# An attention and expert kernel: gathered rows turned by DMA instead of by TensorE, with a new order of the last two feed-forward units

## What is computed

```python
x = x + xattn_ffn(layernorm(x), ctx)   # causal self-attention, attention on ctx,
                                       # feed-forward 256 -> 1024 -> 256 (ReLU), each with add + layernorm
h = layernorm(x)
probs = softmax(h @ wg.T)              # 8 experts
topk_w, topk_idx = top_k(probs, 2);  topk_w /= sum(topk_w)
h1, h3 = h @ w1[e], h @ w3[e]          # 256 -> 512
y_e = (silu(h1) * h3) @ w2[e]          # 512 -> 256
x = x + sum over the two experts of topk_w * y_e
```

## Time and profile before

| | |
|---|---|
| median of 3 runs | 536.51 us (534.71 to 536.86) |
| profiled execution | 538.54 us, of it span 536.7 us |
| PE busy | 500.5 us (93%) |
| PEld | 326.6 us (61%) |
| DVE | 378.5 us (71%) |
| ACT | 286.5 us (53%) |
| POOL | 288.0 us (54%) |
| expert tiles, from the first ups | from 353.50 us on |

### The profile page before, as it was taken

The page is one execution under the profiler, slowest core; times in us unless marked ns, Lnnn a source line. Parts: engine busy times, 40 slices in busy tenths (PEclk is TensorE's granted clock), DMA queues, the critical chain, the costliest instruction groups (busy, mean ns, idle before and its releaser), DMA issues.

```text
span 536.7 us, 10988 instructions
## 1 busy us (share of the span) xinstructions
PE 500.5 (93%) x3686; PEld 326.6 (61%) x3686; DVE 378.5 (71%) x968; ACT 286.5 (53%) x574; POOL 288.0 (54%) x324
## 2 busy tenths in 40 slices
PE   7999999999899999898999988899998999999990
PEld 3676766666667666566666764556655656666660
DVE  6899887588877678858977989788857544444440
ACT  4556867655648637654647557455544334433430
POOL 4464112004724519936696875343566665766663
PEclk9899999999999999999999999899999999999996
DMA  8002534246887357763697770226885677878973
GB/s 278 7 31 70 171 94 120 84 107 118 145 173 143 109 110 132 160 165 109 106 213 158 145 259 11 69 65 124 142 155 100 116 120 136 126 126 123 139 91 40
DMA packets 135314, 65.61 MB, mean 122 GB/s; under 512 B 109757, under 2 KB 126590, under 8 KB 135262
## 3 DMA queue, kind: packets, MB, share of 16 engines
q1 hardware_dynamic: 127774, 54.69, 45.9%
q0 software_dynamic: 7488, 10.23, 12.8%
HBM read 28.19 MB, written 10.35 MB: 72 GB/s over the span
## 4 chain that ended last, share of the span: by engine, by line
PE 51%; DVE 16%; DMA 11%; issue 8%; ACT 6%; POOL 4%; POOLq 2%; SPq 1%; DVEq 0%; ACTq 0%
PE ps L1197 41%; DMA out<-y,qst 6%; DMA probT<-prob 3%; PE ps L1292 3%; PE ps L1294 3%; PE ps L1293 3%; DVE cmax L1735 2%; ACT ps L1008 1%; POOL y L935 1%; DVE tT L1944 1%; POOLq L955 1%; DVE prob L1876 1%; DVE arena L394 1%; POOL out L961 1%; DVE arena L468 1%
## 5 line engine op out<-in xcount | busy, mean ns | idle before, releaser
L1197 PE MATMUL ps<-arena,probT 128*128 128x256 f16 (+2 forms) x1092 | 179.6, 318 | 3.5 <-DMA probT<-prob 2.2
L1197 PEld LDWEIGHTS ps<-arena,probT 128*128 128x128 f16 (+1 forms) x1092 | 104.8, 97 | 60.7 <-issue 7.0
L961 POOL DMA_INDIRECT out<-y,qst x39 | 62.7, 1608 | 23.6 <-DMA out<-y,qst 12.9
L1197 PE MATMUL ps<-arena,qT 128*128 128x512 f16 (+1 forms) x384 | 68.9, 332 | 1.6 <-DVE prob L1876 1.2
L1007 ACT ACTIVATE prob<-ps,nbias 128x512 f16<-128x512 f32 x64 | 39.0, 609 | 53.3 <-DVE nbias L1741 53.3
L2296 DVE SCALAR_TENSOR_TENSOR ps<-ps,w1m 128x512 f32<-128x512 f32 x39 | 27.4, 703 | 53.5 <-ACT w1m L1138 51.0
L1138 ACT ACTIVATE w1m<-ps 128x512 f32<-128x512 f32 x39 | 23.3, 597 | 76.9 <-PE ps L1197 63.8
L1197 PE MATMUL ps<-arena,tT 128*128 x468 | 57.3, 273 | 0.6 <-DVE tT L2395 0.6
L776 POOL TENSOR_TENSOR rstd<-veps,expo 128x1 f32<-128x1 f32 x16 | 9.2, 573 | 88.0 <-DVE veps L1770 88.0
L1197 PEld LDWEIGHTS ps<-arena,qT 128*128 128x128 f16 x384 | 32.4, 97 | 37.1 <-issue 3.2
L1197 PE MATMUL ps<-w2s,tT 128*128 128x256 f16 x384 | 47.6, 274 | 3.4 <-DVE tT L1944 3.0
(11 more groups left out here) (232 smaller groups left out, 920.4 us busy)
## 6 DMA issues: line engine op xcount, KB each, us to landing
stage<-we_in SPq DMA_DIRECT2D x33, 256.0 KB, 3.1
prob<-we_in SPq DMA_DIRECT2D x15, 256.0 KB, 3.7
xin<-x_in SPq DMA_DIRECT2D x16, 128.0 KB, 2.8
out<-y SPq DMA_DIRECT2D x16, 128.0 KB
hrow<-tT SPq DMA_DIRECT2D x4, 512.0 KB, 3.3
y<-x_in SPq DMA_DIRECT2D x3, 512.0 KB, 7.2
stage<-z_in SPq DMA_DIRECT2D x4, 256.0 KB, 5.5
prob<-w_in SPq DMA_DIRECT2D x4, 256.0 KB, 2.8
```

Of the source, the lines that this page charges most:

```text
L961: g.indirect_dma_start(out[:rows_of(p), :], bass.IndirectOffsetOnAxis(ridx[:, n:n + 1], 0), ys[:, n % RING, :], None, compute_op=ALU.add). ...
L1197: r = t.matmul(o, lhs(a), rhs(b), start=first and n == 0, stop=last and n == 2)
```

## The change

Gathered rows are no longer turned by PE and copied by ACT: SP issues a DMA transpose of 128x512 float16 (`x_turn(n)`) into a ring of four slots in `w1m`, where the feed-forward weights lay. Because of that, the first four turns wait for the last `up`. In SP's order `x_turn(n + 4)` stands ahead of `act_turn(n)`. `gather(n)` waits for `x_turn(n - 4)`, `e_ups(n)` for `x_turn(n)`. AHEAD is 8, but gathers of a new phase wait for iteration 3 and 11, and one iteration issues two at most. In the feed-forward of blocks 2 and 3, PE's and DVE's order is rewritten, and `h_trans(2)` and `logits(2)` stand behind the last `down` and behind `e_ups(0)`.

```diff
-RING, AHEAD, BEHIND = 4, 6, 3
-LEAD = 2
+RING, AHEAD, BEHIND = 4, 8, 3
+GATHERS_FROM = {1: 3, 2: 11}
+MOST = 2
...
-        xT = ph[:, 4096:5120].rearrange("p (q b c) -> p q b c", q=2, b=2 * KD)
+        xT = w1m[:, 2 * NI:].bitcast(F16).rearrange("p (s b c) -> p s b c", s=RING, b=2 * KD)
...
+            def x_turn(n):
+
+                s = n % RING
+                if n < RING:
+                    wait(sp, "f_up", KF * NB)
+                else:
+                    wait(sp, "e_up", n - RING + 1)
+                wait(sp, f"e_x{s}", 16 * (n // RING + 1))
+                sp.dma_start_transpose(xT[:, s], xg[:, s, :]).then_inc(sm[f"e_t{s}"], 16)
+
...
             store_h(sp, 2)
+            for n in range(RING):
+                x_turn(n)
             for n in range(NJ):
+                if n + RING < NJ:
+                    x_turn(n + RING)
                 if n < NJ - 1:
                     act_turn(n)
...
-                    wait(pool, "e_xtr", n - RING + 1)
+                    wait(pool, f"e_t{n % RING}", 16 * (n // RING))
...
-            issued = AHEAD - 1
+            issued = 5
             for n in range(NJ):
-                while issued < min(NJ, n + AHEAD + (LEAD if n > PHASES[2][1] - AHEAD + 1 else 0)):
-                    gather(issued)
-                    issued += 1
+                for _ in range(MOST):
+                    if issued < min(NJ, n + AHEAD) and n >= GATHERS_FROM.get(phase_of(issued), 0):
+                        gather(issued)
+                        issued += 1
...
-                    if u == NB - 1 and f == 6:
-                        h_hi(2)
...
             ffn(NB - 1)
+            h_hi(2)
-
-            def x_copy(n, q):
-                act_.wait_ge(sm["e_xtr"], n + 1)
-                copy(xT[:, q, :, :].rearrange("p b c -> p (b c)"), x_bank(n)).then_inc(sm["e_xcp"], 1)
...
-            def x_trans(n, s):
-                pe.wait_ge(sm[f"e_x{s}"], 4 * (n - s) + 16)
-                for b in range(2 * KD):
-                    r = t.transpose(x_bank(n)[:, b * P:(b + 1) * P], xg[:, s, b * P:(b + 1) * P],
-                                    ident16[:])
-                r.then_inc(sm["e_xtr"], 1)
...
-                pe.wait_ge(sm["e_xcp"], n + 1)
+                s = n % RING
+                pe.wait_ge(sm[f"e_t{s}"], 4 * (n - s) + 16)
...
-            make_lists(0)
             down(3, 2)
             up(3, 5)
             down(3, 3)
             up(3, 6)
+            make_lists(0)
             down(3, 4)
...
             down(3, 7)
-            logits(2)
+            wait(pe, "r_list", 1)
+            h_trans(2, 0)
+            h_trans(2, 1)
             wait(pe, "f_lo", KF * NB)
             wait(pe, "st_lo", G_FF + len(rest))
-            wait(pe, "e_xcp", 2)
             e_ups(0, 0)
+            logits(2)
...
             rest_los(3, 3)
+            hid_lo(3, 5)
+            list_read(0)
+            rest_los(3, 4)
+            hid_lo(3, 6)
             for m in range(TB):
                 x1_stats(2, m)
             x1_aggr(2)
...
+            rest_los(3, 5)
+            hid_lo(3, 7)
+            rest_los(3, 6)
             h_norm(2)
...
+            rest_los(3, 7)
             h_lo(2)
```

More of the change, by code:

```diff
@@ L322, in xattn_ffn_moe @@
             h_out x1_out fill_out r_count r_tab r_next r_made r_listed r_list chain links_p
-            e_x0 e_x1 e_x2 e_x3 e_a0 e_a1 e_a2 e_a3 e_xtr e_xcp e_up e_sil e_act e_ahi e_alo e_down e_y
+            e_x0 e_x1 e_x2 e_x3 e_a0 e_a1 e_a2 e_a3 e_t0 e_t1 e_t2 e_t3 e_up e_sil e_act e_ahi e_alo e_down e_y
             e_add0 e_add1 e_add2 e_add3 e_ltr e_lcp""".split()
@@ L1144, in act_hi, with e_step @@
                 copy(arow[:, s, 0, :], ps[2 * (s % 2) + 1][:]).then_inc(sm["e_ahi"], 1)
-            def e_step(n, s, nxt=True):
+            def e_step(n, s):
                 silu(n, s % 2)
-                if nxt:
-                    x_copy(n + 1, 1 - s % 2)
                 act_hi(n, s)
@@ L1183, in _ @@
             for n in range(E_LOOP, NJ):
-                e_step(n, n % RING, n + 1 < NJ)
+                e_step(n, n % RING)
             wait(act_, "e_ltr", 1)
@@ L1501, in _ @@
             down(2, 2)
+            up(2, 5)
             pe.wait_ge(sm["c_u"], NT)
@@ L1544, in e_ups @@
                     for k in range(KD):
-                        r = mm3(ps[2 * q + h][:], lambda a: xT[:, q, a * KD + k, :],
+                        r = mm3(ps[2 * q + h][:], lambda a: xT[:, s, a * KD + k, :],
                                 lambda b: ew[:, at + (k * 2 + h), b, :], k == 0, k == KD - 1)
@@ L1573, in _ @@
             down(3, 5)
-            wait(pe, "f_lo", KF * NB - 2)
-            x_trans(0, 0)
-            wait(pe, "r_list", 1)
-            h_trans(2, 0)
             down(3, 6)
-            wait(pe, "f_lo", KF * NB - 1)
-            x_trans(1, 1)
-            h_trans(2, 1)
             wait(pe, "r_tab", 1)
@@ L1584, in _ @@
             down(3, 7)
-            logits(2)
+            wait(pe, "r_list", 1)
+            h_trans(2, 0)
+            h_trans(2, 1)
             wait(pe, "f_lo", KF * NB)
             wait(pe, "st_lo", G_FF + len(rest))
-            wait(pe, "e_xcp", 2)
             e_ups(0, 0)
+            logits(2)
             wait(pe, "n_u", NT)
-            x_trans(2, 2)
             wait(pe, "r_lg", NB - 1)
             e_ups(1, 1)
-            x_trans(3, 3)
             ranks(2)
@@ L1604, in routing_read, with e_step @@
                 wait(pe, "r_used", j - (NB - 3) + 1)
-            def e_step(n, s, nxt=True, between=None, banks=None):
+            def e_step(n, s, between=None, banks=None):
                 q = s % 2
@@ L1613, in e_step @@
                     between()
-                if nxt:
-                    x_trans(n + 1, (s + 1) % RING)
                 if n == BEHIND + 1:
@@ L1637, in _ @@
             for n in range(2, E_LOOP):
-                e_step(n, n % RING, n > 2, work.get(n), read.get(n - 1))
+                e_step(n, n % RING, work.get(n), read.get(n - 1))
             for n in range(E_LOOP, NJ - 1):
@@ L2243, in _ @@
             table_counts(0)
+            place(1)
             hid_lo(2, 5)
@@ L2246, in _ @@
             rest_los(2, 5)
-            place(1)
             table_starts(0)
             hid_lo(2, 6)
+            hid_lo(2, 7)
             rest_los(2, 6)
+            y_lo(NB - 1)
+            rest_los(2, 7)
             table_keys(0)
-            table_experts(0)
-            hid_lo(2, 7)
-            rest_los(2, 7)
-            y_lo(NB - 1)
             for m in range(TB):
                 out_tile(2, m)
+            hid_lo(3, 0)
             for m in range(TB):
                 out_stats(2, m)
-            hid_lo(3, 0)
             out_moments(2)
+            hid_lo(3, 1)
+            table_experts(0)
+            rest_los(3, 0)
+            hid_lo(3, 2)
             centre(2, range(TB))
-            rest_los(3, 0)
-            hid_lo(3, 1)
             rows_hot(1)
-            rest_los(3, 1)
-            hid_lo(3, 2)
+            hid_lo(3, 3)
             tiles_hot(0)
             spread_vals(0)
+            rest_los(3, 1)
+            hid_lo(3, 4)
             rest_los(3, 2)
-            hid_lo(3, 3)
             rest_los(3, 3)
+            hid_lo(3, 5)
+            list_read(0)
+            rest_los(3, 4)
+            hid_lo(3, 6)
             for m in range(TB):
@@ L2275, in _ @@
             x1_aggr(2)
-            hid_lo(3, 4)
-            list_read(0)
-            rest_los(3, 4)
-            hid_lo(3, 5)
+            rest_los(3, 5)
+            hid_lo(3, 7)
+            rest_los(3, 6)
             h_norm(2)
-            rest_los(3, 5)
-            hid_lo(3, 6)
+            rest_los(3, 7)
             h_lo(2)
-            rest_los(3, 6)
-            hid_lo(3, 7)
-            rest_los(3, 7)
             table_rest(0)
```

12 lines of the change are left out of this document (removed).

## The result

The changed kernel takes 545.61 us (median of 4 runs, 544.75 to 546.44), the kernel before on the same chip 536.68 (534.71 to 538.89). The medians lie 8.9 us apart. Ratios here leave out executions more than 1.5% above their kernel's fastest. The ratio is 1.0144, with a 95% interval of 1.0098 to 1.019: slower, by 7.7 us (5.3 to 10.2). The profiled execution took 546.44 us with a span of 544.7.

What follows compares the result with a forecast made beforehand. POOL's row of gathers, adds and landings was taken to set the end, with PE only keeping ahead. Terms 0, +0.9, -1.9, +2.9 and 0 sum to +1.9 us, 538.5 on the 536.51 median; range 531 to 546.

Steps and rivals of the forecast that it cites:

- rival B: DMA transposes crowd out POOL's adds: 23 waits grow by 0.75 us each, 553 us; half gives 546; chance 0.20.
- Transposes off PE are worth 0: Expert loop: PE saves 0.22 us a tile, 8.6 in all, but POOL's row of adds covers it, so 0.
- no wait for a weighted tile after the first: Expected trace sign in the expert loop: POOL waits some 23 times for adds, never for a later weighted tile.
- Start +0.9: Front of the expert loop: the first add starts later by 0.1 to 1.5 us, taken as +0.9.
- my signs: Expected trace times at the front: first ups near 350, `dl` 355 to 357, first downs 366.5 to 368, first add 369.4 to 371.
- so `dl` stays at 355.00: Front, DVE: logits of block 2 behind 2.6 us of ups come at 352.9, when they ran before, leaving `dl` unchanged.
- up to half of 2.8 us: Front, PE: first ups falling into a low-clock stretch would lose up to 1.4 us.
- Gathers' order -1.9: POOL, iteration 13: one gather instead of three ahead of an add wins 1.3 to 2.6 us, taken as -1.9.
- Within 4.5: Expected trace sign: iteration 13's add follows the one before within 4.5 us in place of 5.8.
- DMA load +2.9: POOL's row: added DMA transposes lengthen each of 23 add waits by at most 0.25 us, 0 to +5.7, taken as +2.9.

Runs made afterwards that it cites:

- the order alone: Kernel before with only the new order of the gathers, TensorE still turning the rows; ratio 0.9981, -1.0 us.
- the load alone: Kernel before plus one idle 128x512 DMA transpose behind each activation's transpose, awaited by no engine but SyncE at slot reuse; ratio 1.014, +7.5 us.
- the run with the activation first: Changed kernel with each activation's transpose issued ahead of the turning of rows four tiles on in SyncE's queue; 546.19 us, ratio 1.0135.

## Why the prediction was right, and where it was off

The range (531 to 546) holds 545.6 by 0.4 us, and slower was the likeliest sign; the time itself was 7 us too low. The sum's own bounds, 534 to 542.5, do not hold it: what does is the reach up into rival B. The sum had +0.9 for the start and -1.9 + 2.9 = +1.0 for the row; the traces have +3.1 and +4.9. So the sign and the mechanism of the row were right, and that the time fell inside is in part luck. Step by step:

1. **Transposes off PE are worth 0**: right, as far as the runs can tell. With three of four left out PE's side gave nothing, and with all of them gone PE stood idle 13.5 us in the loop. The sign "no wait for a weighted tile after the first" failed, not because PE's work counted, but because its inputs came late.
2. **Start +0.9** (bounds +0.1 to +1.5): the step that failed in its working; measured +3.1. First ups at 350.1 were right to 0.3 us, but first downs (369.16) and first add (372.38) came later than the 366.5 to 368 and 369.4 to 371 of my signs. Wrong was "so `dl` stays at 355.00" (356.73): I moved logits behind ups at full clock, and put the low clock in as a loss of its own at the end, when it stands ahead of logits. Its price was wrong too: "up to half of 2.8 us", when products at the lower level can take nearly twice as long (downs of 2.74 us in place of 1.47, below) and lose nearly all of it. They lost 1.96, and 1.37 more in a second stretch that I didn't have. And I did not name what is queued behind the logits on DVE: block 2's ranking, and behind it tile 0's `gated`, for which PE stood 2.58 us ahead of that second stretch. The chain I did follow, from `gather(4)` over `x_turn(4)` to `act_turn(0)`, exists and cost 0.94 us.
3. **Gathers' order -1.9**: measured -1.0, with an interval of -2.7 to +0.6. The interval of iteration 13 shrank as I wrote, but less than I wrote: from 5.80 to 5.22 us here and 4.04 with the order alone. "Within 4.5" held only there; with the new order of blocks 2 and 3 beside it, and no transposes, it is 4.58.
4. **DMA load +2.9** (0 to +5.7): the mechanism was right and its size too small; the load alone measured +7.5. The first adds said 0.49 us for 1.50 of transposes and the gathers, so at most 0.25 a wait, and I halved that again, "since not every add meets a transpose". In the runs 0.75 us of idle transposes a tile costs the whole 0.25 in a mean landing and about 0.3 in a wait. The sum also lacked the second way in which the turning reaches POOL: I followed SyncE's queue for the first tile only. In the loop, too, `act_turn` stands behind an `x_turn` that waits for its gather (37.6 us), PE waits 12.6 us for it, and 5.2 us of waits for a weighted tile reach POOL. Taking the queue away moved these waits and not the time.

The Trainium skill's rule ("VectorE: DVE Perf Modes", Rules for kernel authors), TensorE for a 128x128 block whose destination can be PSUM and DMA only otherwise, points the right way here, though not by its prices of one block: 39 turnings by DMA cost 8.3 us net, 0.21 a tile, not the 5.2 less 1.6 that my estimate from its figures would give as time. The cost is not the transpose's own duration, which lies four tiles ahead of its use, but what it does to the transfers beside it.

Rival B, crowding out, had its deciding point at 0.25 us a wait; the runs show 0.25 to 0.3, and the time is that of its half, 546. That it is so near is in part chance: half of B is all row, and here 3.1 of the 8.0 us lie in the start. Still, I gave that half less than I should have. The Trainium skill's sentence that each DMA engine serves its queues in turn ("DMA: Bandwidth & Descriptors", Queues, rings and completion order) goes with that: the adds were slowed by 0.2 to 0.3 us for each dose, not stopped for the whole 0.75, and twice the load gave about twice the loss in time.

## What to carry to other kernels

Taking work from the busiest engine helps only if that engine ends last, and where two stand close (here 157 and 159 us), a resource that both use decides: each extra transfer of 128 KB a tile cost 0.2 us a tile with nobody waiting for it. So price a move onto the DMA engines by what the latency-bound transfers beside it lose, and test it first with idle transfers, which takes ten lines. When an operation is moved behind another on one engine, list what stands behind its result on the next engine, and count a low clock ahead of it, at up to twice the time. Where one queue issues two kinds of transfers, ask at every tile, and not at the first alone, what the first kind waits for.

## What the hardware showed that I had not expected

- The DMA engines' load costs long before they are full: -0.75, +0.75 and +1.5 us of their time a tile gave -2.7, +7.5 and +14.6 us, with the share at 0.78 in the kernel before. The lower arm is short, probably because PE then holds (7.4 us of waits for weighted tiles).
- A plain copy of 128 KB, 144 packets by the page's totals, disturbed the adds about as much as a transpose of 544 (the totals less the 135314 of before, over 38).
- Waits of PE of 2.84, 1.21 and 1.37 us with little work between them were followed by a granted clock of 0.52 over 7 us, in which twelve products of 512 columns took 4.71 us, and a wait of 2.58 by one of 0.50 over 3 us; yet in the run with the activation first a wait of 2.57 at the same place was followed by full clock. Later a wait of 4.53 for an activation was followed by downs of 2.74 us in place of 1.47:

```profile
432.91 2.74 PE L1193 MATMUL ps<-arena,tT 128*128 x12 [4.53 <-DMA tT<-prob]
```
